# Local attention layers: three of four low parts made on POOL, and other weights waited for at the first output projection

## The reference, cut to what matters

```python
def _layer(x, wqkv, qs, ksc, wo, lg, lb, w1, b1, w2, b2):
    h = shift_token(x)          # channels 64..127 come from the token before
    q, k, v = split(h @ wqkv)   # 8 heads of 64
    q = l2norm(q) * qs; k = l2norm(k) * ksc
    q, k = rotary_xpos(q, k)
    o = local_attention(q, k, v)    # windows of 64 tokens, looking one window back
    x = x + o @ wo
    h = layernorm(shift_token(x)) * lg + lb
    a, g = split(h @ w1 + b1)
    return x + (a * gelu(g)) @ w2 + b2
```

## Time and profile before

| what | value |
| --- | --- |
| median of three timed runs | 1738.26 us |
| lowest and highest of them | 1727.55 and 1738.48 us |
| the profiled execution's own time | 1739.82 us |
| its span from first to last instruction | 1738.0 us |
| TensorE busy | 1556.5 us, 90% of the span |
| DVE, ACT, POOL busy | 1359.7, 1183.2 and 627.1 us |
| both local layers | from about 455 to 906 us of the span |

### The profile page before, as it was taken

The page is one execution under the profiler, slowest core; times in us unless marked ns, Lnnn a source line. Parts: engine busy times, 40 slices in busy tenths (PEclk is TensorE's granted clock), DMA queues, the critical chain, the costliest instruction groups (busy, mean ns, idle before and its releaser), DMA issues. The chain is left out here.

```text
span 1738.0 us, 29422 instructions
## 1 busy us (share of the span) xinstructions
PE 1556.5 (90%) x11136; PEld 853.3 (49%) x11136; DVE 1359.7 (78%) x1905; ACT 1183.2 (68%) x2296; POOL 627.1 (36%) x510
## 2 busy tenths in 40 slices
PE   6699999996679888698897999999998999999998
PEld 4122222221457665466753233333335778888786
DVE  4899999992577645877356999999974988999986
ACT  4368888886368753587635488878863877777775
POOL 2810000000467660667413133222221455555555
PEclk9689999999589988799998799999997999999999
DMA  2420011000111110011003321111010111111111
GB/s 77 109 92 20 19 22 32 5 1 1 71 25 32 32 32 19 19 32 32 17 8 94 107 69 23 29 23 29 5 14 10 50 44 43 49 43 49 44 48 50
DMA packets 68284, 66.05 MB, mean 38 GB/s; under 512 B 40840, under 2 KB 44296, under 8 KB 67632
## 3 DMA queue, kind: packets, MB, share of 16 engines
q1 hardware_dynamic: 67504, 61.94, 13.5%
q10 hardware_dynamic: 576, 2.16, 0.3%
q0 software_dynamic: 64, 0.07, 0.0%
HBM read 40.85 MB, written 14.81 MB: 32 GB/s over the span
## 5 line engine op out<-in xcount | busy, mean ns | idle before, releaser
L942 ACT ACTIVATE att_probs<-psum 128x512 f32<-128x512 f32 x1024 | 532.3, 604 | 167.2 <-PE psum L844 164.8
L958 DVE TENSOR_REDUCE att_neg_max<-psum 128x1 f32<-128x1024 f32 x512 | 600.9, 1219 | 35.4 <-PE psum L812 31.2
L812 PE MATMUL psum<-att_k_op,att_q_op 48*128 48x512 bf16 x1024 | 343.6, 406 | 17.3 <-DVE att_neg_max L958 10.6
L844 PE MATMUL psum<-att_q_op,att_k_op 50*128 50x512 bf16 x1024 | 316.1, 389 | 24.6 <-ACT att_probs L942 24.4
L2126 ACT ACTIVATE moe_hidden<-psum,moe_b 128x512 f32<-128x512 f32 x256 | 167.1, 690 | 83.9 <-PE psum L68 83.7
L844 PEld LDWEIGHTS psum<-att_q_op,att_k_op 50*128 50x128 bf16 x1024 | 77.6, 94 | 272.3 <-ACT att_probs L942 215.6
L862 PE MATMUL psum<-att_probs,att_v 128*32 128x512 f32 (+2 forms) x1664 | 203.3, 558 | 2.9 <-ACT att_sums L928 2.8
L61 DVE TENSOR_TENSOR moe_hidden_low<-moe_hidden,moe_hidden_high 128x512 fp32r<-128x512 f32 x192 | 198.7, 1082 | 6.2 <-ACT moe_hidden_high L2134 6.0
L1047 POOL TENSOR_TENSOR att_diag<-att_probs,att_triangle 128x512 f32<-128x512 f32 x64 | 81.1, 1266 | 278.8 <-ACT att_probs L942 142.1
L2184 POOL TENSOR_TENSOR moe_hidden_low<-moe_hidden,moe_hidden_high 128x512 fp32r<-128x512 f32 x64 | 99.0, 1547 | 166.7 <-ACT moe_hidden_high L2134 166.7
L812 PEld LDWEIGHTS psum<-att_k_op,att_q_op 48*128 48x128 bf16 x1024 | 74.1, 95 | 129.1 <-DVE att_neg_max L958 107.8
(11 more groups left out here) (261 smaller groups left out, 2850.6 us busy)
## 6 DMA issues: line engine op xcount, KB each, us to landing
moe_spread_weights<-gate_rows SPq DMA_DIRECT2D x64, 256.0 KB, 3.2
wl_v_shift<-wl_v SPq DMA_DIRECT2D x62, 128.0 KB, 2.2
att_q_op<-qk_parts SPq DMA_DIRECT2D x32, 192.0 KB, 3.4
att_k_op<-qk_parts SPq DMA_DIRECT2D x32, 192.0 KB, 4.4
qk_parts<-att_hi SPq DMA_DIRECT2D x12, 256.0 KB, 4.0
qk_parts<-att_hi SPq DMA_DIRECT2D x12, 192.0 KB, 2.9
att_q_op<-att_neg_rows SPq DMA_DIRECT2D x128, 2.0 KB
qk_parts<-att_mid SPq DMA_DIRECT2D x8, 256.0 KB, 3.2
```

The source lines that it names most:

```text
L812: mm = pe.matmul(buf[:, half * CHUNK:(half + 1) * CHUNK], q_op[it % RING][at_rows(p, MAX_ROW), j, t * P:(t + 1) * P], k_op[it % RING][at_r ...
L844: pe.matmul(st_bank[e % 3], k_op[it % RING][at_rows(p, MAX_ROW + 2), j, t * P:(t + 1) * P], q_op[it % RING][at_rows(p, MAX_ROW + 2), j, ha ...
L942: act.activation(probs[:, g % PB, h, :], st_bank[e % 3], ACT.Exp, scale=scale).then_inc(exp_done, 1)
L958: dve.tensor_reduce(neg[:, t, 2 * p + j:2 * p + j + 1], ring[e % 2], AX.X, ALU.max, negate=True).then_inc(ring_free, 1)
```

## The change

It has two parts. First, TensorE's wait for `weights_loaded` moves from ahead of slot 0 into slot 8, just ahead of `project_o(0)`. Second, DVE no longer makes the low parts of chunks 1, 2 and 3; POOL does, at the start of its slots 1, 2 and 3. They count up a semaphore of their own, `win_h_low_rest`, for which TensorE waits at tiles 4, 8 and 12. Chunk 0 stays on DVE, and ACT's high parts stay where they were (the table `split_at` has the same slots).

```diff
+    split_at = {1: 1, 2: 2, 3: 3}
...
             def project_q(i):
-                pe.wait_ge(h_low_done, 2 * (i // 4 + 1))
+                if i < 4:
+                    pe.wait_ge(h_low_done, 2)
+                else:
+                    pe.wait_ge(h_low_rest, 2 * (i // 4))
                 if i:
                     pe.wait_ge(q_rotated, 3 * i)
                 project(i, 0, q_bank).then_inc(q_ready, 1)
...
-            pe.wait_ge(s.weights_loaded, 16 * LAYER_WEIGHTS * (l + 1))
             pe.wait_ge(cleared, 1)
             for n in range(SLOTS):
...
                 if n < TILES:
                     project_k(n)
+                if n == LAG_Y:
+                    pe.wait_ge(s.weights_loaded, 16 * LAYER_WEIGHTS * (l + 1))
                 if LAG_Y <= n:
                     project_o(n - LAG_Y)
...
         @block.scalar
-                if 1 <= n < CHUNKS:
-                    split_h(n)
+                if n in split_at:
+                    split_h(split_at[n])
...
         @block.vector
             for n in range(SLOTS):
-                if 1 <= n < CHUNKS:
-                    split_h(n)
...
         @block.gpsimd
+            def split_h(c):
+                at = slice(c * CHUNK, (c + 1) * CHUNK)
+                pool.wait_ge(q_added, n)
+                pool.wait_ge(k_added, n)
+                if n > LAG_V:
+                    pool.wait_ge(q_scaled, n - LAG_V)
+                    pool.wait_ge(k_scaled, n - LAG_V)
+                pool.wait_ge(h_high_done, 2 * c + 1)
+                low_part(pool, s.h_low[0:half, at], s.y[0:half, at], s.h_high[0:half, at]).then_inc(h_low_rest, 1)
+                b0 = int(c % 2 == 0)
+                lo, hi = c * CHUNK + b0, (c + 1) * CHUNK
+                pool.wait_ge(h_low_rest, 2 * c - 1)
+                pool.wait_ge(h_high_done, 2 * c + 2)
+                low_part(pool, s.h_low[half:P, lo:hi], s.y[half:P, lo - 1:hi - 1], s.h_high[half:P, lo:hi])\
+                    .then_inc(h_low_rest, 1)
+                pool.wait_ge(h_low_rest, 2 * c)
+
             for n in range(TILES + LAG_S):
+                if n in split_at:
+                    split_h(split_at[n])
                 if LAG_V <= n < TILES + LAG_V:
```

More of the change, by code:

```diff
@@ L1186, in window_layer @@
     NT = len(HID_TILES)
+    split_at = {1: 1, 2: 2, 3: 3}
     upcoming = prologues[l + 1] if l + 1 < DEPTH else None
     with (rearmed(nc, *(f"{n}_{l}" for n in (
-                  "win_h_high", "win_h_low", "win_cleared", "win_q_ready", "win_k_ready", "win_v_ready", "win_q_squared",
+                  "win_h_high", "win_h_low", "win_h_low_rest", "win_cleared", "win_q_ready", "win_k_ready", "win_v_ready", "win_q_squared",
                   "win_k_squared", "win_q_rotated", "win_k_rotated", "win_q_reduced", "win_k_reduced",
@@ L1196, in window_layer @@
                   "ffn_gelu", "ffn_gated", "ffn_out", "ffn_y_added")), *(f"win_v_shifted{r}_{l}" for r in range(V_RING))) as
-          (h_high_done, h_low_done, cleared, q_ready, k_ready, v_ready, q_squared, k_squared, q_rotated, k_rotated,
+          (h_high_done, h_low_done, h_low_rest, cleared, q_ready, k_ready, v_ready, q_squared, k_squared, q_rotated, k_rotated,
            q_reduced, k_reduced, rooted, floored, inverted, q_added, k_added, q_scaled, k_scaled, q_turned,
```

## The result

The changed kernel took 1723.11 us in the median of 15 runs (1717.34 to 1727.18), against 1738.21 us (1726.37 to 1739.14) before. The ratio is 0.992 with a 95% interval of 0.9907 to 0.9932: 15.1 us, 0.9%, faster. The profiled execution took 1725.98 us, with a span of 1724.2 us where 1738.0 stood.

What follows compares the result with a forecast made beforehand. DVE was taken to set the pace in slots 0 to 3. The moved wait's 3.6 us and the low parts' 8.1 us sum to 11.7, taking the median from 1738.26 to a forecast 1727 us, range 1715 to 1736.

Steps and rivals of the forecast that it cites:

- The moved wait: Start of each layer: first projection 0.15 us behind the last memset, gaining 2.18 and 1.44 us, together 3.6; free at slot 8.
- The low part's price: POOL's slots 1 to 3: 1.27 us for one low part, 1.25 where POOL runs without a pause.
- The rule that made 1.27 the choice over 2.42: DVE locks ports shared with POOL only with two SBUF inputs; slots 1 to 3 have none, so POOL is undisturbed.
- POOL as the pace: Slots 1 to 3: POOL's 5.0 us a slot sets the pace, under the old 5.86; DVE waits for it.
- without a pause: POOL from slot 1 to slot 4: 12 pieces of 1.25 us, 15.0 us, its waits for its own results costing nothing.
- Key transposes: First key transposes of the two layers: about 5.9 and 5.8 us earlier.
- To the layers' ends: From slot 5 on: the gain stands to the end of the layer and of the kernel, 11.7 us in all.
- rival 2: Slots 5 to 8: the clock's rise keeps its time, up to 3 us a layer is lost; 1733 us, chance 0.13.
- Rival 4: Layer start and POOL's chain: hidden waits remain, so within 1 us of before, 1738; chance 0.03.
- rival 3: POOL's slots 1 to 3: gain gone at 2.24 us a low part, about 1740 us at 2.42; chance 0.04.
- a change within 1%: Whole kernel: time differs from before by less than 1%, 17 us, likely sign faster; chance 0.83.
- rival 1: TensorE's clock rises sooner, by slot 4, as projections stand closer: 6 us more gain, 1721 us; chance 0.12.

Runs made afterwards that it cites:

- e1: The kernel before with only the wait for the weights moved from ahead of slot 0 to slot 8; median 1728.87 us, ratio 0.9951.
- e5: The changed kernel with low parts of chunks 1 to 3 shared, channels 0 to 63 on POOL, 64 to 127 on DVE; median 1722.29 us, ratio 0.9945.
- e7: The changed kernel with low parts of chunks 2 and 3 made by DVE in slots 5 and 6; median 1724.52 us, ratio 0.9928.
- e2: The changed kernel with the wait for the weights back ahead of slot 0, so only the low parts moved to POOL; median 1728.28 us, ratio 0.9948.
- e4: The changed kernel with each of POOL's low parts computed twice; median 1739.45 us, ratio 1.0018 against the kernel before.
- e6: The kernel before with a delay of DVE memsets ahead of layer 1's slots; median 1743.3 us, ratio 1.005.
- e9: The changed kernel with POOL's low parts in slots 1, 6 and 8, plus DVE memsets as delay ahead of layer 1; median 1729.19 us, ratio 0.9967.

## Why the prediction was right, point by point

**The moved wait.** Forecast 2.18 and 1.44 us; e1's ramps gained 2.73 and 1.52. The start itself is as said: the projection follows the end of the last memset by 457.58 - 457.52 = 0.06 us in the profile after, not 0.15, which with 2.81 and 2.07 us before makes 2.27 and 1.53 us of start. What is over in layer 0 is clock. At slot 8 no wait for the weights is seen, as said.

**The low part's price.** 1.27 us was taken, 1.28 and 1.09 measured for the two of a pair, 1.18 in the mean (1.22 with the wait between them); on half the partitions a subtraction takes as long as an addition on all, or 0.2 us less. The rule that made 1.27 the choice over 2.42 was borne out: nothing on DVE in slots 1 to 3 has two inputs in SBUF, and no piece of POOL takes over 1.30 us. e5 and e7, which put such an instruction back on DVE, have 1.54 for 1.28 and 2.95 for 2.04. The Trainium skill's factor of 2 ("GPSIMD Engine Reference", section "Engine selection") would have made 1.38 of DVE's 0.69, an estimate; the measured factors are 1.85 and 1.58.

**POOL as the pace.** Forecast 5.0 us a slot, measured 5.16. The term that was mis-sized is POOL's wait for its own results: 0.13, 0.08 and 0.08 us a slot, 0.29 together, set at nothing. The shorter low parts (2.36 us a pair for 2.50) gave half of it back, and over three slots 0.4 to 0.45 us are left, by which the chains of the changed kernel and of e2 are longer than 15.0. So "without a pause" holds for other engines' work alone. The forecast inferred "no gap" from instructions of one kind that follow each other with no such wait between. e4 shows that the pace is POOL's, with 7.5 and 7.4 us for 7.3. DVE waits for it in slots 2 and 3, as the forecast had it.

**Key transposes.** Forecast 5.93 and 5.76 us earlier, measured 5.60 and 5.44. The 0.3 us of each are the chain's 0.4, less the 0.09 by which the start was earlier than forecast.

**To the layers' ends.** The gain stood, but the exact agreement is in part luck. Ramp and step to the first addition together are 128.66 us before and 117.20, 116.76 and 116.84 in three executions after: 11.5 to 11.9 us, against 11.7 forecast. Of that, 11.0 us are ramps; the rest is clock in the step to the first addition, which happens to make up for POOL's own waits. And it hangs on the one profiled execution of before: with e6's layer 0 in its place (62.31 us for 64.73), 9.0 to 9.5 us are left.

The granted clock rose for good at 492.7 us before. The windows view of the changed kernel has it full from 485.5 us on:

```profile
485.50:492.70 7.20, 5.49 (x54) 3.31 (x53) 5.06 (x11) 5.80 (x13) 5.47 (x5) 1.00 0.16 36
```

Counted from the last memset that is 28.5 us in place of 35.5, a rise earlier by more than the 5.6 us of work. But e6, with before's list, has its full clock from 486.7 us on, which is 29.3 us. So the profiles do not show that the closer work brought the rise. Nor is rival 2 shut out: against before's execution the step to the first addition is not longer in layer 0 and 0.2 us longer at most in layer 1, but against e6's it is 1.4 us longer in layer 0, about half of what the rival had for a layer. The prediction's "0.50 until 492.7 us" was itself misread: the windows view of the kernel before has 0.60 from 475 to 480 us and 0.74 from 480 to 485. No term rests on it. Rival 4 had no place, and rival 3 needed a part of twice the price.

**The sum.** 1727 was forecast and 1723.1 measured, a change within 1%, the case that had a chance of 0.83. The figure is nearer to rival 1's 1721 than to the forecast, but the steps do not bear out the rival's reason. Of the 13.8 us between the two profiled spans, 11.5 are these steps, 1.7 lie in the feed-forward part of layer 0 and 0.4 behind the local layers; the remaining 0.2 lie ahead of the first memset. The 1.7 us are clock, not list. From the last output addition to the first feed-forward addition it is 26.47 us before and 24.70 after. The windows of that stretch, the first 0.5 us short of it (columns as in the earlier trace rows):

```profile
640.00:666.00 26.00, 22.70 (x93) 16.61 (x92) 15.20 (x23) 9.44 (x16) 11.78 (x8) 0.80 0.00 1
```

```profile
633.50:658.20 24.70, 21.07 (x94) 15.10 (x94) 15.34 (x24) 9.45 (x16) 11.77 (x8) 0.86 0.00 1
```

The same work, at a mean clock of 0.80 and 0.86; neither later profile of the changed kernel has this gain. So this is not rival 1, which had the clock rise for good because of closer work. In slots 1 to 3 the clock did rise early in places (products at 0.39 us from 465 to 471 us), and there it bought nothing, because POOL was the pace.

The medians differ by 15.1 us, more than the sum of these steps. 62 of 93 executions of the kernel before took 1736 us or more and 23 under 1730, so its median lies in the upper group; the changed kernel's are spread evenly over 1714 to 1727. The means, 1735.5 and 1722.5, differ by 13.0. Over e1 to e9, means follow the ramps and the steps to the first addition within about 3 us. What sets the share of executions in each group was not settled: e6 and e9 show only that a delay of 7 to 9 us comes through nearly whole.

## What to carry to other kernels

Price a move to a slower engine by that engine's whole list in the slot. 2.4 us on POOL, and 0.2 of waits around them, for 2.1 on DVE was a gain because 5.2 us were still less than 5.9, and it ends where the new engine becomes the pace. Look for the gaps of the engine that takes the work, not only of the one that gives it: by the steps, slots 6 and 8 held a pair of low parts for nothing, slot 10 cost 1 us, and DVE's idle time in slots 5 and 6 was no free room, with POOL busy beside it. Where single executions differ by 7 to 13 us, judge changes of some us by steps between fixed instructions in the trace, take the steps of before from more than one execution too, and expect a median to move by more or less than they do.

## What the hardware showed that was not expected

DVE and POOL hold each other up in both directions when DVE's instruction has two SBUF inputs: 0.69 us became 1.28 on DVE and 1.28 became 1.54 on POOL (e5). The stretch behind the local layers takes 823 to 834 us with one and the same list there; of the 7.2 us between before and e1, 4.9 arise after a point at which the granted clock, over 40 us, is 0.78 in the one and 0.96 in the other. Where POOL waits for its own last result, 0.08 to 0.14 us stand between two instructions (changed kernel and e2), while additions without such a wait follow each other with no gap. The same subtraction on 64 partitions took POOL 1.28 us for channels 0 to 63 and 1.09 for channels 64 to 127.
